# Which of two TensorE programs stands behind the FFN's branch

## The reference

```python
gate_wq = jax.random.randint(ks[1], (I, H), -128, 128, dtype=jnp.int32)   # I = 1376, H = 512
...
gate_w = _dequant(gate_wq, gate_scale)
up_w = _dequant(up_wq, up_scale)
down_w = _dequant(down_wq, down_scale)
gate = jax.nn.silu(jnp.einsum('bsh,ih->bsi', x, gate_w))
up = jnp.einsum('bsh,ih->bsi', x, up_w)
intermediate = gate * up
return jnp.einsum('bsi,hi->bsh', intermediate, down_w)
```

## Time and profile before

| | before |
|---|---|
| three runs | 1474.76 us median, 1473.42 to 1476.17 |
| the profiled execution | 1474.53 us |
| its span, first to last instruction | 1472.6 us |
| mean granted TensorE clock | 0.995 of full speed |
| TensorE busy | 1423.7 us, 97% of the span |
| attention 0's end to the FFN's first product | 372 to 386 us |
| FFN 0's products on TensorE | 386 to 524 us |
| attention 1 and FFN 1 | 524 us to the end |

### The profile page before, as it was taken

How to read it: one execution, slowest core, us unless ns; L and a number is a source line. 1 busy time by engine, 2 the same in 40 slices (tenths; PEclk the granted TensorE clock), 3 DMA queues, 4 the chain that set the end, 5 groups by cost and what they waited for, 6 DMA issues and landing times.

```text
span 1472.6 us, 30227 instructions
## 1 busy us (share of the span) xinstructions
PE 1423.7 (97%) x8737; PEld 1252.0 (85%) x8737; DVE 1026.6 (70%) x2516; ACT 890.6 (60%) x2444; POOL 783.5 (53%) x827
## 2 busy tenths in 40 slices
PE   6999999999899989999999999999999999999997
PEld 4899999998577767898898898898889889889786
DVE  3899999998777675656656655656665665665865
ACT  3788888888454536565655555655565555556611
POOL 3455555555321127856657556566576565664521
PEclk9999999999999999999999999999999999999999
DMA  5433333321345401010010110100101111000200
GB/s 177 148 91 94 92 100 91 91 75 49 95 136 157 122 8 58 30 57 28 29 56 28 52 33 28 57 28 28 57 28 42 43 28 57 28 28 29 79 22 36
DMA packets 56104, 92.83 MB, mean 63 GB/s; under 512 B 6016, under 2 KB 27008, under 8 KB 56064
## 3 DMA queue, kind: packets, MB, share of 16 engines
q1 hardware_dynamic: 56064, 92.33, 21.1%
HBM read 81.82 MB, written 2.10 MB: 57 GB/s over the span
## 4 chain that ended last, share of the span: by engine, by line
PE 59%; POOL 2%; DVE 2%; issue 1%; DMA 0%; ACT 0%; POOLq 0%; SPq 0%; DVEq 0%
PE c_bv L101 7%; PE c_bv L102 7%; PE c_bv L103 7%; PE c_bx L101 4%; PE c_bx L103 4%; PE c_bx L102 4%; PE c_by L101 3%; PE c_by L102 3%; PE c_by L103 3%; PE c_bt L1853 3%; PE c_bs L1843 1%; PE c_bs L101 1%; PE c_bo L103 1%; PE c_bo L1863 1%; PE c_bs L103 1%; PE c_bo L101 1%
## 5 line engine op out<-in xcount | busy, mean ns | idle before, releaser
L531 POOL TENSOR_TENSOR h_pr<-h_pr,h_rinv 128x512 f32<-128x512 f32 x128 | 133.2, 1041 | 144.4 <-DVE h_rinv L657 142.1
L1423 POOL TENSOR_TENSOR c_qk<-g_y,c_qk 128x512 fp32r<-128x512 f32 x96 | 124.0, 1292 | 144.7 <-ACT c_qk L1524 144.7
L1284 POOL TENSOR_TENSOR b_sw_lo<-b_slots,b_sw_hi 128x512 fp32r<-128x512 f32 (+1 forms) x128 | 148.5, 1160 | 10.2
L1282 POOL CAST b_sw_hi<-b_slots 128x512 fp32r<-128x512 f32 (+1 forms) x128 | 72.9, 569 | 135.0 <-DMA b_slots<-in_w_qk 134.6
L101 PE MATMUL c_bv<-b_wv_hi,g_xT_hi 128*128 128x256 f32 x504 | 141.0, 280 | 0.0
L102 PE MATMUL c_bv<-b_wv_lo,g_xT_hi 128*128 128x256 f32 x504 | 140.9, 280 | 0.0
L103 PE MATMUL c_bv<-b_wv_hi,g_xT_lo 128*128 128x256 f32 x504 | 140.7, 279 | 0.0
L1524 ACT ACTIVATE c_qk<-g_y 128x512 fp32r<-128x512 f32 x96 | 60.9, 634 | 105.1 <-DVE g_y L1659 74.7
L1624 DVE TENSOR_TENSOR c_bo<-c_bo,g_wo 128x128 f32<-128x128 f32 x128 | 38.3, 299 | 120.7 <-ACT g_wo L1499 119.8
L568 ACT ACTIVATE h_pr<-h_bs,h_nmax 128x256 f32<-128x256 f32 x256 | 119.2, 479 | 2.5 <-DVE h_nmax L652 2.4
L1489 ACT ACTIVATE c_pr<-c_pr,c_rinv 128x128 f32<-128x128 f32 (+1 forms) x256 | 101.8, 448 | 8.2 <-DVE c_rinv L1614 8.2
(11 more groups left out here) (379 smaller groups left out, 5200.1 us busy)
## 6 DMA issues: line engine op xcount, KB each, us to landing
f_wi<-in_w_ffn SPq DMA_DIRECT2D x66, 256.0 KB, 2.7
b_slots<-in_w_qk SPq DMA_DIRECT2D x64, 256.0 KB, 3.0
a_w<-in_w_head SPq DMA_DIRECT2D x28, 352.0 KB, 2.9
h_part<-in_w_ffn SPq DMA_DIRECT2D x32, 264.0 KB, 2.7
h_o_mix<-h_o_hi SPq DMA_DIRECT2D x64, 128.0 KB, 2.2
b_raw_v<-in_w_v SPq DMA_DIRECT2D x16, 512.0 KB, 4.7
b_raw_o<-in_w_o SPq DMA_DIRECT2D x16, 512.0 KB, 4.4
b_ffn_w<-in_w_ffn SPq DMA_DIRECT2D x4, 576.0 KB, 5.6
```

What stands on the lines that cost most here:

```text
L531: pool.tensor_tensor(pr[b][:, :, :], pr[b][:, :, :], rinv[b][:, :][:, :, None].to_broadcast([P, 2, S]), ALU.mult)\
L1282: pool.tensor_copy(self.sw[0][:, a:b], self.slots[:, a:b]).then_inc(self.s_whi, 1)
L1284: pool.tensor_tensor(self.sw[1][:, a:b], self.slots[:, a:b], f32(self.sw[0][:, a:b]), ALU.subtract)\
L1423: pool.tensor_tensor(lo, src, f32(hi), ALU.subtract).then_inc(s_sumlo, 1)
```

## The change

The condition of the branch and the two bodies trade places. The If body is now the program with two matmuls per weight block, the Else body the one with three. Which program runs for a given input stays the same, since the number is an integer.

```diff
             largest = pe.value_load(g["largest"][0:1, 0:1])
-            with pe.If(largest > EXACT):
+            with pe.If(largest < EXACT + 1):
+                exact[0] = True
                 all_rounds()
             with pe.Else():
-                exact[0] = True
+                exact[0] = False
                 all_rounds()
```

## The result

Over 21 executions each, on the same chips, the changed kernel took 1478.39 us (median, 1475.91 to 1480.31) and the kernel before 1475.52 us (1472.94 to 1477.87). The ratio is 1.0019, with a 95% interval of 1.0013 to 1.0026: some 2.8 us more. The ratio is just inside the 0.2% which the prediction took for no difference, though its interval reaches past it, and the time is inside the range. It is 1.1 us more than the forecast's 1.75, and this 1.1 us is the interesting part.

The account below looks back on a forecast made before the run. TensorE, busy 97% of the span, was taken to bound the kernel. 0 at the start plus 1.75 us at the end, on 1474.53 and then the 1474.76 median, gave 1476.5 us, 0.12% more; range 1474.3 to 1478.8.

Parts of the forecast that it names:

- the forecast's 1.75: Block's end: TensorE's new far jump opens the barrier 1.75 us later, paid in full; chance of this forecast 0.56.
- The ratio within 0.2%: Whole kernel: time differs from before by under 0.2%, 2.95 us, taken as indistinguishable from no change; chance 0.74.
- the clock rival: Behind the end's jump: idle TensorE's clock falls, products slow, 2.15 us on top of 1.75, 1478.7 us; chance 0.17.
- the prediction's own signs of being wrong: Profile after: short jump at the end, first FFN product not near 386.2, or low clock behind 525.
- Start, what is removed: Start: branch falls through, projections come sooner, but transposes still wait for VectorE's normalisation at 378.84; 0 us.
- Start, the clock: Start: clock falls again at much the same place, 0 us; bounds 1.8 us gained and 1.4 us lost.
- The bound of 1.8 us: Start: gain if TensorE's clock stayed full through transposes and output product; as a rival, chance 0.11.
- End, the jump: Block's end: far jump takes 3.6 us, partly hidden by the drain's wait, so the barrier opens 1.75 us later.
- The bound of 0.2 us: Block's end: lower bound of the jump's length, hidden under the drain, adding 0; nearly free jump's chance 0.12.
- that of 7.2 us: Block's end: upper bound of the jump's length, two blocks fetched one after the other, adding 5.35 us; chance 0.04.
- the sum of 0: Whole kernel: total if the end's jump took the skill's 51 ns and hid under the drain, instead of 1.75 us.
- End, the clock: Behind the end's jump: clock as before, nowhere low near 526, since 1.7 us of dense products separate two idle times.

Follow-up runs that it names:

- the kernel before, filled: Kernel before plus matmuls nobody reads in the start's idle times: 1474.0 us, 0.9988; with 9 more ahead of the last down product: 1473.4 us, 0.9985.
- the wait filled: Changed kernel plus 9 matmuls nobody reads in TensorE's wait ahead of the last down product: 1478.49 us, 1.0020 to the kernel before.
- short Else: Changed kernel with the never-run Else body cut to one last down product, so the end's jump is short: 1475.37 us, 0.9997 to the kernel before.
- jump taken early: Changed kernel with the last down product moved behind the branch into its own small branch, far jump reached earlier: 1476.52 us, 1.0005 to the kernel before.
- the changed kernel with a filled start: Changed kernel plus 10 and 9 matmuls nobody reads behind the projection pairs at the start: 1474.8 us, 0.9998 to the kernel before.

## Why the prediction was right, and where it was not

The ratio within 0.2% was forecast with 0.74, and it came out so, but narrowly: with an interval that reaches 1.0026, this is partly luck. The measured difference of 2.8 us lies midway between the forecast (1.75) and the clock rival (3.9). And one of the prediction's own signs of being wrong came true: a low clock behind 525.

*Start, what is removed: right.* The branch fell through in 68 ns, the second pair waited for its copy, the transposes for the layer norm, with the idle 2.14 us in front of them that was worked out as 2.1. Counted from the write of the largest magnitude, the transposes stand at 380.36 − 373.29 = 7.07 us, and at 378.84 − 371.78 = 7.06 before. Removing the far jump bought nothing by itself, and the fillers say nearly the same from the other side: the kernel before, filled, has a start of 12.9 to 13.1 us with the far jump in it, the changed one 12.6.

*Start, the clock: right in the mean, wrong in that it was told as one answer.* Over the eight profiles of the new form whose start was not filled the start was 13.6 to 15.1 us, 14.2 in the mean, beside 14.44 in the one profile of before. The low stretch came in all, but 3.4 us long in some and 6.8 in others and at different places: the three starts of 13.6 to 13.7 us have the short one, the five from 14.05 up the long one. A gain of 0.2 us in the mean can't be told from chance. The bound of 1.8 us for a clock that stays full was good: filled starts gained 1.3 to 1.8.

*End, the jump: right.* Forecast 3.6 us for the jump and 1.75 for the barrier; measured 3301 and 3604 ns in the two profiles of the changed kernel, and 1.63 and 1.68 us at the end where nothing was filled there and no clock fell. The bound of 0.2 us was the price of a short jump (174 ns), and that of 7.2 us was nowhere. By the Trainium skill, Advanced Engine Details and Errata, section Control Flow Timing, an unconditional branch takes about 51 ns; the traces, which list the jump as a COMPARE_BRANCH, give 174 ns for a short one and 3.3 us or more for the far one. So the sum of 0 that went by that figure was wrong here.

*End, the clock: here a term was missing.* The rival "the clock falls behind the end's jump" was priced somewhat high (2.15 us; measured 10.08 − 8.52 = 1.56 us between two executions of the same kernel, and 10.23 − 8.52 = 1.71 with the wait filled) and given too little chance, 0.17. The step that failed is the one that said the clock would be as before at this place, because the same 2.20 us idle had kept 1.00 in the earlier trace rows and 1.7 us of dense products lay between the two idle times. Two things are wrong with it. The row was one execution of something that differs between executions: 2.20 us idle also lost the level, in the kernel before with fillers only at the start. The other row that had kept it, the stretch from 533.0 to 538.8, did no better: counted from ScalarE's value split, the eight later falls came in that stretch or within 1.2 us behind it. And dense products in between don't protect: with 1.7 us of them and the earlier wait filled as well, the level fell behind 2.09 us idle.

How the 1.1 us beyond the jump comes about is argued and not shown. At 1.6 us for a fall, the changed kernel would need one in two of three executions more than the kernel before; that is an estimate worked backwards from the times, not counted. Six profiles have the far jump at the end with one idle time or both unfilled, and four of them show a fall. But in three of these it began at 523.3 to 523.5, ahead of the jump's idle time, with the same wait that the kernel before has ahead of it; and of the four profiles with that wait and no jump behind it (before, short Else, jump taken early, before with the start filled) two show one as well, for 1.4 and 1.5 us. What agrees over all executions is the mean clock: 1.6 us' worth less, of which 1.1 us would have to fall on working time.

What remains open: how often the clock falls at this place in each kernel, the one before included, since only the profiled execution shows where; and whether it was chance that the changed kernel with a filled start showed none up to the value split, since its end has the same two idle times.

## What to carry to other kernels

A jump over a thousand instructions to code that has not run yet held TensorE's sequencer for 3.3 to 4.1 us, and cost only what no queued work or other wait covered; put it where the array has work queued or waits for something else, never right ahead of a barrier. Look at what it leaves TensorE idle for, since a fall of the clock behind an idle time is a second price, here about as large as the first (1.6 and 1.65 us). And a row that shows the clock kept across an idle time is one draw: look at the same place in several executions before the sum leans on it.

## What the runs showed of the hardware

The price of a far jump varied between 3279 and 4081 ns over the profiles, and not with the distance: over some 2,100 instructions it was 3339, over 1,060 it was 3279 to 3747 in the other kernels that jump ahead of the barrier. A short jump took 174 to 190 ns, a branch that fell through 67 to 86.

The same program loses TensorE's clock at a given place in one execution and keeps it in another (ends of 10.08 and 8.52 us), and idle times of 2.09 and of 2.20 to 2.35 us were enough for it to be lost. Products whose results nobody reads, put into waits, made the kernel before 1.7 us faster at the start alone and 2.0 us with the wait ahead of the last down product, two gains that the intervals don't tell apart.
